# Reciprocal square root on ACT in place of square root and DVE reciprocal, in a four-layer conv/attention/expert kernel

## The reference, cut to what matters

```
x = L0_conv(x, ...)                               # position and channel attention
x = x + L1_conv(_gn(x), ...)                      # group norm, mask, 3x3 convolution
t = _to_tokens(x)
t = t + L2_attn(_ln_t(t), ...)                    # LN_ATT2
t = t + L2_ffn(_ln_t(t), ...)                     # LN_FFN2: 8 experts, the best 2 of a token
t = t + L3_attn(_ln_t(t), ...)                    # LN_ATT3; inside it two more norms, LN_MID3 and LN_END3
t = t + L3_ffn(_ln_t(t), ...)                     # LN_FFN3: 16 experts, the best 4 of a token, and a shared one

def _ln_t(v, eps=1e-05):
    m = jnp.mean(v, axis=-1, keepdims=True)
    s = jnp.var(v, axis=-1, keepdims=True)
    return (v - m) / jnp.sqrt(s + eps)
```

## Time and profile before

| what | before |
| --- | --- |
| runs | 383.86 us median (383.23 to 385.24) |
| profiled execution, its span | 383.78 us, 382.0 us |
| PE busy | 364.0 us (95% of the span) |
| DVE busy | 183.4 us (48%) |
| ACT busy | 112.3 us (29%) |
| granted PE clock | 1.00 in every stretch |
| chain that ended last | PE 73%, DVE 13%, POOL 4% |

### The profile page before, as it was taken

The page is one execution under the profiler, slowest core; times in us unless marked ns, Lnnn a source line. Parts: engine busy times, 40 slices in busy tenths (PEclk is TensorE's granted clock), DMA queues, the critical chain, the costliest instruction groups (busy, mean ns, idle before and its releaser), DMA issues.

```text
span 382.0 us, 14474 instructions
## 1 busy us (share of the span) xinstructions
PE 364.0 (95%) x5883; PEld 281.8 (74%) x5883; DVE 183.4 (48%) x565; ACT 112.3 (29%) x216; POOL 32.0 (8%) x88
## 2 busy tenths in 40 slices
PE   8989889998999999998999999999999999999995
PEld 3637655775465566653459999999999999999994
DVE  1682756326586576779523333433334333333432
ACT  2500536354323743152112222222222222222220
POOL 7504000000000000000771000000000000000000
PEclk9999999999999999999999999999999999999999
DMA  8694000360000000002995000778887877027300
GB/s 297 239 182 81 0 2 2 101 228 2 0 2 2 2 2 1 2 0 98 346 357 202 17 7 7 227 237 260 278 276 258 273 234 234 7 78 262 122 2 29
DMA packets 39809, 47.33 MB, mean 124 GB/s; under 512 B 1725, under 2 KB 33642, under 8 KB 39658
## 3 DMA queue, kind: packets, MB, share of 16 engines
q1 hardware_dynamic: 39130, 45.81, 38.4%
q0 software_dynamic: 512, 1.12, 0.8%
q10 hardware_dynamic: 144, 0.09, 0.2%
HBM read 42.55 MB, written 4.47 MB: 123 GB/s over the span
## 4 chain that ended last, share of the span: by engine, by line
PE 73%; DVE 13%; POOL 4%; issue 3%; DMA 3%; ACT 2%; SPq 1%; POOLq 0%; DVEq 0%; ACTq 0%
PE bank L1176 26%; PE bank L1195 13%; PE bank L809 4%; PE bank L799 4%; POOL sorted_rows L598 4%; PE bank L881 3%; PE bank L610 3%; PE bank L695 2%; DVE late_room L1720 2%; DMA sorted_rows<-token_rows,row_no 2%; PE bank L718 1%; PE bank L707 1%; PE bank L1138 1%; PE bank L1134 1%; PE bank L1139 1%
## 5 line engine op out<-in xcount | busy, mean ns | idle before, releaser
L1948 DVE TENSOR_TENSOR shared_room<-bank,shared_room 128x512 f32<-128x512 f32 (+1 forms) x63 | 40.7, 647 | 59.2 <-PE bank L1176 59.2
L1176 PEld LDWEIGHTS bank<-shared_room,late_room 128*64 128x64 f32 x1936 | 57.9, 138 | 1.6 <-issue 1.6
L1176 PE MATMUL bank<-shared_room,late_room 128*64 128x64 f32 x1936 | 58.4, 222 | 0.5 <-issue 0.5
L1371 ACT ACTIVATE shared_room<-bank 128x512 f32<-128x512 f32 (+1 forms) x63 | 35.4, 562 | 66.1 <-PE bank L1176 66.1
L1176 PE MATMUL bank<-shared_room,w 128*64 128x64 f32 x1760 | 53.1, 222 | 0.0
L1176 PEld LDWEIGHTS bank<-shared_room,w 128*64 128x64 f32 x1760 | 52.7, 138 | 0.2 <-issue 0.2
L610 PE MATMUL bank<-ones_bf 128*128 128x512 bf16 x144 | 35.1, 387 | 1.4 <-POOL ones_bf L518 1.4
L1956 DVE SCALAR_TENSOR_TENSOR ye_lo<-bank,slot_weight,ye_hi 128x128 fp32r<-128x128 f32 x21 | 7.4, 350 | 57.7 <-ACT ye_hi L1375 57.7
L1195 PEld LDWEIGHTS bank<-late_room,shared_room 128*64 128x64 f32 (+1 forms) x484 | 26.4, 137 | 4.3 <-issue 4.3
L1375 ACT ACTIVATE ye_hi<-bank,slot_weight 128x128 fp32r<-128x128 f32 x21 | 7.7, 368 | 73.9 <-PE bank L1195 73.9
L1195 PE MATMUL bank<-late_room,shared_room 128*64 128x128 f32 (+1 forms) x484 | 29.3, 275 | 0.0
(11 more groups left out here) (372 smaller groups left out, 448.4 us busy)
## 6 DMA issues: line engine op xcount, KB each, us to landing
late_room<-in_w SPq DMA_DIRECT2D x16, 682.5 KB, 5.3
w<-in_w SPq DMA_DIRECT2D x16, 682.5 KB, 5.3
late_room<-in_w SPq DMA_DIRECT2D x8, 640.0 KB
w<-in_w SPq DMA_DIRECT2D x8, 640.0 KB
sorted_rows<-blank SPq DMA_DIRECT2D x1, 3014.0 KB, 19.0
shared_room<-in_experts SPq DMA_DIRECT2D x8, 257.0 KB, 5.8
l<-in_l SPq DMA_DIRECT2D x1, 1422.0 KB, 8.6
w<-in_sw SPq DMA_DIRECT2D x2, 682.5 KB
```

The costliest lines, as they stand in the source:

```text
L1176: last = mm(bank[b][r:r + HALF, to:to + HALF], w[p][x][:, 128 * t + r:128 * t + r + HALF], xe[:, p, HALF * x:HALF * x + HALF], start=True, ...
L1371: nc.scalar.activation(silu[:, slot, 0:n], bank[slot][:, 0:n], ACT.Silu)\
L1948: tt(he[:, p, t0:t1, :].rearrange("p t s -> p (t s)"), bank[2 + slot][:, 0:n], silu[:, slot, 0:n], ALU.mult).then_inc(sem("he_ready"), 1)
```

## The change

All seven square roots of the norms become reciprocal square roots (`Abs_reciprocal_sqrt`), on ACT, with the same operands, as do the one-element activations that load the table. `newton` loses its first operation, the reciprocal on DVE, and reads ACT's result as its first estimate. Its three other operations stay. The tile `lr0` is no longer written.

```diff
-            nc.scalar.activation(nothing[:], ones[0:1, 0:1], ACT.Sqrt).then_inc(sem("table_loaded"), 1)
+            nc.scalar.activation(nothing[:], ones[0:1, 0:1], ACT.Abs_reciprocal_sqrt).then_inc(sem("table_loaded"), 1)
             act.wait_ge(sem("table_loaded"), 2)
             act.wait_ge(sem("gvar_ready"), 1)
-            nc.scalar.activation(gr[:, 0, :], gvar[:], ACT.Sqrt).then_inc(sem("gsd_ready"), 1)
+            nc.scalar.activation(gr[:, 0, :], gvar[:], ACT.Abs_reciprocal_sqrt).then_inc(sem("gsd_ready"), 1)
...
             def deviation(k):
 
-                prepare(ACT.Sqrt)
+                prepare(ACT.Abs_reciprocal_sqrt)
                 act.wait_ge(sem("lmv_ready"), k + 1)
-                nc.scalar.activation(lsd[:, k, :], lmv[:, k, :, 1], ACT.Sqrt, bias=eps[:]).then_inc(sem("lsd_ready"), 1)
+                nc.scalar.activation(lsd[:, k, :], lmv[:, k, :, 1], ACT.Abs_reciprocal_sqrt, bias=eps[:]).then_inc(sem("lsd_ready"), 1)
...
-            def newton(r, r0, sd, v, tmp):
-
-                settle(nc.vector.reciprocal(r0, sd))
+            def newton(r, r0, v, tmp):
+
                 settle(tt(tmp, r0, r0, ALU.mult))
                 settle(stt(tmp, tmp, -0.5, v, ALU.mult, ALU.mult))
                 settle(stt(r, tmp, 1.5, r0, ALU.add, ALU.mult))
...
-            newton(gr[:, 2, :], gr[:, 1, :], gr[:, 0, :], gvar[:], gr[:, 3, :])
+            newton(gr[:, 2, :], gr[:, 0, :], gvar[:], gr[:, 3, :])
...
-                newton(lr[:, k, :], lr0[:, k, :], lsd[:, k, :], lve[:, k, :], lra[:, k % 2, :])
+                newton(lr[:, k, :], lsd[:, k, :], lve[:, k, :], lra[:, k % 2, :])
```

## The result

The kernel after took 381.82 us, the median of 7 runs (381.02 to 383.08), beside 383.99 us for the kernel before in the same measurement (7 runs, 383.23 to 385.57). The ratio is 0.9935 with a 95% interval of 0.9915 to 0.9955. Two later measurements of the same pair gave 0.9957 (0.9932 to 0.9983) and 0.9960 (0.9938 to 0.9983). So the kernel became faster by 0.4 to 0.65%, 1.5 to 2.5 us, where 1.1 us was forecast, and where the prediction gave a gain of over 0.5% a chance of 0.15.

The account below looks back on a forecast made before the run. The prediction took late DVE chains at five norms and PE's fillers at two to bound the first half, a PE loop the second. 382.0 - 1.13 + 1.78 = 382.65, plus 0.08: 382.7 us; range 381.5 to 384.2.

Parts of the forecast that it names:

- what is removed and where it lies: Seven DVE reciprocals leave the chain, 0.20 us at the group norm and 0.21 us at a layer norm.
- PE's idle times: Ahead of the norm's first product: 1.07, 0.21, 0.84, 0.08 us left at group norm, LN_ATT2, LN_ATT3, LN_FFN3.
- The two gains that drew on the same 0.50 us at LN_FFN3: LN_END3 and LN_FFN3 give 0.21 us each, 0.42 of PE's idle 0.50 us, leaving 0.08.
- Back to back they would take 0.90: Four transposes behind the filler take at least 0.90 us, so LN_FFN2 gains 0.06 us and LN_MID3 0.03.
- the sum of 1.13: Gains of all seven norms added: 0.20 + 0.21 + 0.21 + 0.21 + 0.21 + 0.06 + 0.03 us.
- rival 1: Fillers do not bind; LN_FFN2 and LN_MID3 give 0.21 us each, 1.46 in all, so 382.4 us; chance 0.10.
- Function and table at the same price: ACT's new function costs 0 extra, its table load 1283 ns; rival: dearer function, 384.0 us, chance 0.10.
- no load added: ACT's list keeps its table loads; rival: a load ahead of each copy, about 389 us, chance under 0.01.
- no change in the number of steps: Loop steps as many as before; rival: routing changes, one step more 391.1 us or fewer 374.3 us, chance 0.03.
- some tenths: Three runs of before lie from 383.23 to 385.24 us, so a median was taken to move by some tenths.
- the range: Kernel time from 381.5 us, rival 1 less spread and scatter stage, to 384.2 us, dearer ACT function and a little above.

Follow-up runs that it names:

- experiment 4: Kernel after without the three operations of the Newton step, ACT's estimate used as it is at all seven norms: ratio to before 0.9924.
- experiments 5 and 6: After with an unused reciprocal back at LN_FFN2 and LN_MID3: one execution, 382.68 us; after with three filler products fewer at each: one execution, 383.11 us.
- experiment 3: Kernel after with the reciprocal put back on DVE, its result unused, so only ACT's function differs from before: ratio to before 0.9998.
- before's kind: Five profiles: before three times, after with unused reciprocals at all norms, before with six start fillers; L1096 to the scattered rows' product 48.08 to 49.99 us.
- experiment 8: Kernel after with six filler products at the start in place of five: ratio to before 0.9944, median 382.23 us.
- experiment 12: Kernel after without the Newton step, with fewer filler products at four norms and six at the start: ratio to before 0.9872, median 379.99 us.
- experiment 1: Kernel before, unchanged, profiled a second time: ratio 1.0012, median 384.49 us.
- experiment 7: Kernel after without the Newton step and with 8, 15, 13 and 26 filler products at LN_ATT2, LN_FFN2, LN_MID3 and LN_FFN3: ratio to before 0.9904.

## Why the prediction was right or wrong

**Right: what is removed and where it lies.** The 0.20 to 0.21 us from the start of each reciprocal to the next operation is what each norm gave (0.20 to 0.22). The group norm, LN_ATT2, LN_ATT3, LN_END3 and LN_FFN3 gave it whole, and PE's idle times came out as forecast. The two gains that drew on the same 0.50 us at LN_FFN3 both fitted in.

**Wrong: "Back to back they would take 0.90 (two take 0.45 ..., so four take 0.90), which is 0.06 less".** This step of the prediction failed. It sized the gain at LN_FFN2 at 0.06 and at LN_MID3 at 0.03, and they were 0.21 each; it is 0.33 us of the 0.36 by which the sum of 1.13 fell short of 1.49. Two transposes in 0.45 us was a row that began with a wait: it held the time of one product to come through as well as the distance to the next. Four that are all ready take 0.44 (experiment 4). So DVE's last tile, at 58.76 with a transpose 0.38 behind it, had set the end all along, and experiments 5 and 6 show it from both sides: the reciprocal put back costs its whole 0.21, and three fillers fewer give nothing. The prediction had named this as rival 1, with 382.4 us, and had seen the row that spoke for it (the last tile ends 0.58 us after the filler). It let the chain's bar of L610 outweigh this. In the chain the transposes took more than their least time, and that alone said that something other than PE paced them (the prediction even said so, and then held them to 0.90).

**Right: ACT's side.** Function and table at the same price (experiment 3), no load added, no change in the number of steps. The Trainium skill, page "ScalarE: Activation LUTs", section "What it computes", says that `Rsqrt` has known accuracy issues and advises VectorE's reciprocal followed by a `Sqrt` activation in its place; the kernel before had the same two operations in the other order. How accurate the estimate of `Abs_reciprocal_sqrt` is, these profiles don't tell; the loop had the same number of steps in every profile, with the Newton step or without it.

**Off: the size that was measured.** The first measurement found 2.5 us (0.9935), and 1.49 us is 0.9961, just outside its interval and well inside the two later ones (0.9957 and 0.9960). With 1.49 in place of 1.13 the forecast would still have been a gain of 0.4%, under the 0.5% from which the prediction called the kernel faster. What carried the first measurement beyond that the prediction had put at nothing: it took the rest of the program to be the same from one execution to the next, and the scatter of a median to be some tenths. In the profiled pair the rest is the two draws, 0.87 and 0.40 us, which both fell on the side of after. Profiles of before differ by 1.3 us at the start (22.77 to 24.03 at the group norm) and by 1.6 us at a fall of the clock, and profiles of before's kind by 1.9 us at the rows' transfer. Over all executions about half a microsecond is left beyond the 1.49, and it goes with falls of the clock, which came in 42 of 93 executions of before and 2 of 31 of after. Whether the change itself makes them rarer stays open. The time (381.82) lies in the range, and so does what the mechanism alone gives, 383.86 - 1.49 = 382.4; the 0.5 us between them is nothing that the prediction had forecast.

## What to carry to other kernels

A filler in the chain of waits is not proof that it binds. Ask whether what stands behind it takes its least time, and take that least time from a row where all inputs were ready, not from one that begins with a wait. When an effect is near 1 us in 380, compare stretches between fixed instructions of two profiles before reading anything into the ratio. Here they repeat to 0.03 us but for two, one with a fall of the clock (1.56 us longer) and one in experiment 8 (0.17 us longer at LN_ATT3, cause not looked into). Look also at the granted clock of all executions and not only of the profiled one, and take a second profile of the kernel before, which here moved 0.9 us of the supposed gain to chance. Where DVE turns a small result of ACT over, look for the function that gives it turned over already: a DVE operation on 4 elements that waits for the one before it costs 0.19 to 0.21 us of the path, reciprocal or product (rows 4, and 38.45 to 38.64 us in after).

## What the runs showed of the hardware that was not expected

- PE's first products run at the lower clock in every profile (five of 512 columns in 2.29 us, where eighteen take 3.88 later), and the moment at which the clock rises is drawn anew in each execution: its first record lies between 4.29 and 7.81 us, with the same work of PE up to 4.15 us in the kernels with five products. The first products on the input take 1.4 or 1.9 us by it, and the group norm starts up to 1.3 us later.
- One transfer of 68.5 KB from DRAM took some 2 us from issue to landing in eight profiles (1.97 in after) and 3.06 to 3.84 in six, and PE stood up to 2.4 us for it.
- A fall of the clock in mid-program lasted some 3 us and cost 1.4 us (experiment 12) and 1.56 us (experiment 1). It came behind 2.37 us of idle time in the one and behind 0.63 us in the other, yet 2.33 us in experiment 7 and 0.63 us in after were followed by none. Nor were an idle 1.07 us at the group norm and 0.84 us at LN_ATT3, in any profile.
